# The experts' routing and weight loads move into the end of attention

## The reference, cut to what matters

```python
x = L0_attn_a_x                                    # 16 x 512 x 256
x = x + attention(layernorm(x))                    # cos/sin similarities, softmax, values
x = x + experts(layernorm(x), weights, indices)    # 2048 tokens, 2 of 8 experts each
x = x + mamba(layernorm(x))
x = x + experts(layernorm(x), weights, indices)    # the same network and the same indices

# experts: order the 4096 (token, expert) pairs by expert, then for expert e
h  = gelu(xr @ w1A[e].T @ w1B[e])                  # 256 -> 64 -> 1024
ye = h @ w2A[e].T @ w2B[e]                         # 1024 -> 64 -> 256
y[token] += expert_weight * ye
```

## Time and profile before

| | |
|---|---|
| median of three runs | 2811.41 us (2807.35 to 2814.53) |
| the profiled execution | 2807.95 us |
| its span, first to last instruction | 2805.5 us |
| PE busy | 2485.7 us (89%), x15334 |
| DVE busy | 2246.1 us (80%) |
| ACT busy | 1955.1 us (70%) |
| POOL busy | 1932.8 us (69%) |
| granted TensorE clock, mean | 0.956 |

### The profile page before, as it was taken

One profiled execution on the slowest core, in us unless ns is written; L12 is line 12 of the kernel. 1 busy time (PEld: TensorE's weight loads), 2 busy tenths in 40 slices (PEclk: granted clock), 3 DMA queues, 4 the chain that ended last, 5 costly groups with the idle time before them and its releaser, 6 DMA issues. The chain is left out here.

```text
span 2805.5 us, 42277 instructions
## 1 busy us (share of the span) xinstructions
PE 2485.7 (89%) x15334; PEld 1932.2 (69%) x15334; DVE 2246.1 (80%) x2324; ACT 1955.1 (70%) x2809; POOL 1932.8 (69%) x1245
## 2 busy tenths in 40 slices
PE   5999998399688999999999998999999999987894
PEld 4888887366266777677677776777777767767562
DVE  6788875465179898898898988999999999998554
ACT  3656564166478787787877878878889788783562
POOL 1212121142289999899999998988889889897562
PEclk9999999699799999999999999999999999999897
DMA  1212111522223042230422303303123033061234
GB/s 52 68 45 67 45 60 30 118 83 69 73 101 121 9 136 70 68 129 9 135 76 62 129 15 119 96 27 121 49 74 121 10 113 114 2 181 38 65 105 126
DMA packets 143378, 219.70 MB, mean 78 GB/s; under 512 B 27092, under 2 KB 110036, under 8 KB 143188
## 3 DMA queue, kind: packets, MB, share of 16 engines
q1 hardware_dynamic: 135028, 194.91, 22.5%
q0 software_dynamic: 8160, 22.29, 2.9%
HBM read 174.63 MB, written 42.53 MB: 77 GB/s over the span
## 5 line engine op out<-in xcount | busy, mean ns | idle before, releaser
L1508 POOL TENSOR_TENSOR m_state<-m_state,m_c_all 128x1024 f32<-128x1024 f32 x512 | 1199.3, 2365 | 139.1 <-DVE m_state L1615 138.8
L1615 DVE TENSOR_TENSOR_SCAN m_state<-m_decay,m_ps_d 128x1024 f32<-128x1024 f32 x512 | 1152.3, 2274 | 130.6 <-PE m_ps_d L1941 79.0
L1674 ACT ACTIVATE m_decay<-m_dt,m_aneg 128x511 f32<-128x511 f32 x1024 | 663.4, 710 | 20.2 <-DVE m_state L1615 19.4
L1941 PEld LDWEIGHTS m_ps_d<-m_bdiag,m_duT 128*128 128x128 f32 x4096 | 507.1, 197 | 95.6 <-issue 76.3
L1954 PE MATMUL m_ps_y<-k_ident,m_state 128*128 128x128 f32 x4096 | 526.5, 275 | 26.3 <-POOL m_state L1508 26.0
L1941 PE MATMUL m_ps_d<-m_bdiag,m_duT 128*128 128x128 f32 x4096 | 518.1, 281 | 17.6 <-DVE m_state L1615 17.3
L1954 PEld LDWEIGHTS m_ps_y<-k_ident,m_state 128*128 128x128 f32 x4096 | 469.5, 142 | 91.1 <-issue 53.0
L1603 DVE TENSOR_TENSOR m_ps_d<-m_ps_u,m_b_all 128x1024 f32<-128x1024 f32 x256 | 315.6, 1233 | 35.3 <-DMA m_b_all<-m_bc_rows 14.5
L1848 PE MATMUL m_ps_f<-k_w_2a,k_w_1b 128*128 128x512 f32 x512 | 262.6, 639 | 44.5 <-ACT m_up L1762 32.4
L1873 PE MATMUL m_ps_f<-m_up,k_w_1b 128*128 128x512 f32 x512 | 232.0, 596 | 0.7 <-ACT m_up L1762 0.7
L194 POOL TENSOR_TENSOR a_trig_lo<-a_trig,a_trig_hi 128x2048 fp32r<-128x2048 f32 x16 | 75.3, 4708 | 160.4 <-ACT a_trig_hi L356 160.4
(11 more groups left out here) (228 smaller groups left out, 4377.4 us busy)
## 6 DMA issues: line engine op xcount, KB each, us to landing
m_c_all<-m_bc_rows SPq DMA_DIRECT2D x128, 512.0 KB, 5.2
m_b_all<-m_bc_rows SPq DMA_DIRECT2D x64, 512.0 KB, 6.9
out<-m_xw SPq DMA_DIRECT2D x32, 512.0 KB, 3.3
a_xin<-x SPq DMA_DIRECT2D x16, 512.0 KB, 4.6
a_xres<-x SPq DMA_DIRECT2D x16, 512.0 KB, 5.4
x<-a_xout SPq DMA_DIRECT2D x16, 512.0 KB, 3.4
k_w_2a<-x SPq DMA_DIRECT2D x16, 512.0 KB, 8.9
m_xw<-out SPq DMA_DIRECT2D x16, 512.0 KB, 8.8
```

Source lines behind the costliest of these rows:

```text
L1508: nc.gpsimd.tensor_tensor(s, s, c_all[:, n, :, :], ALU.mult).then_inc(weighed, 1)
L1615: nc.vector.tensor_tensor_scan(state[:, r, :, :].rearrange("p n t -> p (n t)"), decay[:, r, :, :].rearrange("p n t -> p (n t)"), ps_d[i % ...
L1674: ins = nc.scalar.activation(decay[:, r, j, 1:S], dt_sb[:, c % DR, 1:S], ACT.Exp, scale=aneg[:, c, n:n + 1])
L1941: ins = nc.tensor.matmul(ps_d[1][:, j, t * P:(t + 1) * P], duT[:, c % DR, t, :], bdiag[:, n // 2, TT * j + t, :], start=True, stop=True)
```

## The change

`attention` only notes its arguments; the first `expert_ffn` calls it as `attention_stage` with the indices and sizes. The routing block and `load_weights` are gone. In their place, inside attention:
- SP loads the indices and expert numbers at the very start, ahead of the first `xin`.
- Step 14 (`NB - 2`): DVE runs `count_pairs` between the angle reduction and `xout`, PE runs the three counting products after the outputs, DVE runs `place_pairs` after `xout`.
- Step 15 (`NB - 1`): DVE runs `mark_slots` after L219, PE runs the 32 list products after the last outputs, DVE runs `list_slots` after the last `xout`. SP issues the loads of `w_2a`, `w_1a` and `w_1b` (nine DMAs) after the load of `xres`, each behind the semaphore that says that attention has no more use for the buffer; after the last store is done it stores the four lists, and waits for the nine loads.
- The instructions of the routing are the same in number, shape and order, and so are their waits on each other, but one: the count waits for all three products, not two. Small tiles of the routing lie in attention's `theta` and `turns`, the large ones in `trig_hi[0]` and `trig_lo[0]`, the products in `ps_t`.
- `w_1a`, `w_1b`, `w_2a` are buffers that outlive attention (`kept1`); `xin`, `xn`, `rest`, `sin_in` and `cos_in` of attention are views of them. The identity is loaded once.
- `w_2b` is loaded at the start of the tiles' block, by SP; PE waits for it before its first use.

```diff
+            sp.dma_start(g_i[:, :, :], indices.rearrange("(t p) k -> p t k", p=P)).then_inc(r_loaded, 16)
+            sp.dma_start(ex_sb[:, :], experts).then_inc(r_loaded, 16)
 
             def emit(st):            # SP
...
                     sp.dma_start(xres[h][:, :, :], rows(x, st.item(0))).then_inc(xres_loaded[h], 16)
+                    if isinstance(st.base, int) and st.item(0) == NB - 1:
+                        sp.wait_ge(xT_full, KT * NB)
+                        sp.dma_start(kept["w_2a"][:, :].rearrange("p (q e) -> p q e", e=ER),
+                                     ROUTE["w2aT"].rearrange("(q p) e -> p q e", p=P)).then_inc(kept_loaded, 16)
+                        sp.wait_ge(reduced, 5 * NB)
...
+                        sp.wait_ge(trig_in_used, 3 * NB)
...
             for h in range(2):
                 sp.wait_ge(stored[h], 16 * (NB // 2))
+            sp.wait_ge(r_list, 4)
+            sp.dma_start(ROUTE["slots"], slots[:, :]).then_inc(r_stored, 16)
+            sp.dma_start(ROUTE["places"], places[:, :]).then_inc(r_stored, 16)
+            sp.dma_start(ROUTE["rows"], pair_row[:, :]).then_inc(r_stored, 16)
+            sp.dma_start(ROUTE["owner"], owner[:, :]).then_inc(r_stored, 16)
+            sp.wait_ge(kept_loaded, 16 * (1 + 2 * KT + 4))
...
             def emit(st):            # DVE
...
+                if isinstance(st.base, int) and st.item(0) == NB - 2:
+                    count_pairs()
+                if isinstance(st.base, int) and st.item(0) == NB - 1:
+                    dve.wait_ge(sim_full, TT * (NB - 1))
+                    mark_slots()
...
+                if isinstance(st.base, int) and st.item(0) == NB - 2:
+                    place_pairs()
+                if isinstance(st.base, int) and st.item(0) == NB - 1:
+                    list_slots()
...
             def emit(st):            # PE, behind the outputs of the step
...
+                if isinstance(st.base, int) and st.item(0) == NB - 2:
+                    pairs = hit.rearrange("p k t e -> p (k t e)")
+                    pe.wait_ge(xT_copied, KT * NB)
+                    pe.wait_ge(r_step, 8)
+                    nc.tensor.matmul(from_p, before_p[:, :], pairs, start=True, stop=True).then_inc(r_pairs, 1)
+                    nc.tensor.matmul(from_all, ones[:, :], pairs, start=True, stop=True).then_inc(r_pairs, 1)
+                    nc.tensor.matmul(ps_t[1][:, NC * E:NC * E + 1], before_p[:, :], ones[:, 0:1], start=True,
+                                     stop=True).then_inc(r_pairs, 1)
+                if isinstance(st.base, int) and st.item(0) == NB - 1:
+                    pe.wait_ge(r_step, 31)
+                    for c in range(NC):
+                        ins = nc.tensor.matmul(from_list, is_lo[:, c, :],
+                                               tok_hi[:, c, :, :].rearrange("p a h -> p (a h)"), start=(c == 0),
+                                               stop=(c == NC - 1))
+                    ins.then_inc(r_pairs, 1)
...
             if first:                # SP in the tiles' block
+                for half in range(2):
+                    sp.dma_start(w_2b[half * R:(half + 1) * R, :, :], w2b.rearrange("(e r) d -> r e d", r=R))\
+                        .then_inc(down_loaded, 16)
```

More of the change, by code:

```diff
@@ L66, in attention, with keep @@
     PI_IN = 3.1415925
+    hold = ROUTE["hold1"] = ExitStack()
+    def keep(name, shape, dt=F32):
+        return hold.enter_context(nc.sbuf_tensor("a_" + name, shape, dt))
+    kept = ROUTE["kept1"] = {"w_1a": keep("w_1a", [P, 2 * KT * ER]), "w_1b": keep("w_1b", [P, ER * FF // P]),
+                             "w_2a": keep("w_2a", [P, FF // P * ER]), "ident": keep("ident", [P, P]),
+                             "slots": keep("slots", [P, NH], I32), "rows": keep("rows", [P, NH], I32),
+                             "places": keep("places", [P, NC], I32), "owner": keep("owner", [1, MT], I32)}
+    r_loaded, r_step, r_pairs, r_list, r_stored, kept_loaded = ROUTE["held1"] = [
+        nc.alloc_semaphore("r_" + n) for n in ("loaded", "step", "pairs", "list", "stored", "kept_loaded")]
+    ROUTE["r_stored"] = r_stored
     with ExitStack() as ctx:
@@ L108, in attention, with room @@
         rden = sb("rden", [P, TT])
+        g_i = sb("g_i", [P, NT, TOPK], I32)
+        ex_sb = sb("experts", [P, E])
+        taken = [0, 0]
+        def room(t, *shape):
+            size = math.prod(shape)
+            flat = (theta, turns)[t][:, :, :].rearrange("p f s -> p (f s)")[:, taken[t]:taken[t] + size]
+            taken[t] += size
+            names = "abcd"[:len(shape)]
+            if len(shape) == 1:
+                return flat
+            return flat.rearrange(f"p ({' '.join(names)}) -> p {' '.join(names)}", **dict(zip(names[1:], shape[1:])))
+        g_f = room(0, NT, TOPK)
+        hit = room(0, TOPK, NT, E)
+        ones, run, before_p = room(0, P), room(0, P), room(0, P)
+        zero_first, count, upto = room(0, E, NC), room(0, E, NC), room(0, E, NC)
+        place_e = room(0, NC, E)
+        tiles, ends, base = room(0, E), room(0, E), room(0, E)
+        place, row_hi, row_lo, column = room(0, NC), room(0, NC), room(0, NC), room(0, 1)
+        list_lo, list_f, token_f, later = room(0, NH), room(0, NH), room(0, NH), room(0, NH)
+        is_hi = room(1, NC, NH)
+        passed, owner_f = room(1, MT, E), room(1, MT)
+        is_lo = trig_hi[0][:, 0:NC * P // S, :].rearrange("p a (c q) -> p (a c) q", q=P)
+        tok_hi = trig_lo[0][:, :, :].rearrange("p a s -> p (a s)")[:, 0:NC * 2 * NH]\
+            .rearrange("p (c a h) -> p c a h", a=2, h=NH)
+        slots, pair_row, places, owner = kept["slots"], kept["rows"], kept["places"], kept["owner"]
         ps_t = [ctx.enter_context(nc.psum_tensor(f"a_ps_t{r}", [P, 512], F32)) for r in range(2)]
@@ L944, in ranks_in @@
             def ranks_in(j, e):
-                if j == 0 and first:
-                    act.wait_ge(w_loaded, 16 * 2 * KT)
                 if j >= 2:
@@ L1067, in _ @@
                     down(j, 0)
-    if not first:
-        ROUTE["hold"].close()
-        held.extend(ROUTE["held"])
+    ROUTE["hold1" if first else "hold"].close()
+    held.extend(ROUTE["held1" if first else "held"])
     nc.clear_and_free_semaphores(held)
```

360 lines of the change are left out of this document (148 added, 212 removed).

## The result

| | before | changed |
|---|---|---|
| median, us | 2812.55 (2803.01 to 2819.51, 8 runs) | 2792.12 (2786.12 to 2801.11, 8 runs) |
| ratio, 95% interval | | 0.9933 (0.9912 to 0.9953), some 19 us |
| profiled execution, its span | 2807.95, 2805.5 | 2791.97, 2790.2 |
| granted clock, mean | 0.956 | 0.961 |

The changed kernel was timed twice more, each time beside the kernel before on one chip: 2785.07 against 2814.89 us (ratio 0.9902, 0.9874 to 0.9929) and 2776.39 against 2800.90 us (0.9913, 0.9897 to 0.9930). The three differences are 20.4, 29.8 and 24.5 us; 24.4 was forecast. In the changed file the lines of the rows ahead are L415 (before L219), L280 (L194), L612 (L407), L635 (L430), L649 (L723), L491 (L290), L253 (L173), L453 (L257), L851 (L830), L862 (L841).

A forecast was written before the change was run, and what follows sets the result against it. A serial 32.6 us stretch between attention and the first network's tiles, a chain beside weight loads nearly as long, was taken as the bound; 29.5 - 5.0 - 0.5 - 0 = 24.0 us off 2811.4 gives 2787.4, named 2787 (range 2779 to 2796).

The forecast's parts named there:

- the tail: From PE's last output product to the tiles' first instruction: 36.7 us shrink to 7.2, gain 29.5 us.
- `place_pairs`: Behind step 14's xout: its small DVE instructions stand still while POOL's L194 runs, so L219 ends 5.0 us later.
- the gathers: Tiles' start: the 1 MB load of w_2b beside the first gathers costs 0, with 2 us as the other bound.
- start, and all before step 14: Program's start: index and expert-number loads ahead of the first xin delay all that follows by 0.5 us (bounds 0 and 2.3).
- rival A: No exclusion for small instructions: place_pairs runs beside POOL's L194; saving 28.5 us, 2783 us; chance 0.13.
- the case that the prediction had named beside the one taken: DVE's scan gets in ahead of L194, POOL starts some 0.7 us later, DVE's next instruction waits: 4.3 to 5.1 us.
- The loads: Attention's last step: nine DMAs (5.2 MB) at 198 GB/s end near 498, before the last store; cost nothing.
- Rivals C and D: C: slow loads hold the block's end, 2800 us, chance 0.04; D: loads at 70 GB/s, slower, 2822 us, chance 0.02.
- one half alone would leave the other to hold the block: Between attention and tiles, 32.6 us: chain and weight loads are nearly equally long; if one left, the other holds the block.
- Rival B: More comes back: list products at half clock, full start cost, slower gathers; saving 16.7 us, 2795 us; chance 0.12.
- Rival E: Attention's loop steps get worse, or moved work waits for something missed; about 2811 us; chance 0.03.
- What the profile would show: Signs: first statistics at about 11 us, tiles 7.2 us after PE's last output product, L219 ending 5 us later.

The follow-up runs named there:

- before_again: The kernel before, unchanged, run for a second trace: 2811.31 us in one run, tiles take 177.71 us.
- before_third: The kernel before, unchanged, run for a third trace; its tiles start at 535.01 us.
- again: The changed kernel once more, nothing edited: 2785.07 us, ratio 0.9902 to the kernel before.
- after_third: The changed kernel, unchanged, for its third trace: 2776.39 us, ratio 0.9913 to the kernel before.
- e1_place_later: The changed kernel with place_pairs moved from step 14 to behind L415 of step 15: 2784.80 us, ratio 0.9894 to the kernel before.
- e2_w2b_early: The changed kernel with w_2b loaded in attention's last step instead of at the tiles' start: 2781.34 us, ratio 0.9886 to the kernel before.
- e5_routing_only: The changed kernel with all weights loaded at the tiles' start, routing kept in attention: 2807.40 us, ratio 0.9969 to the kernel before.
- e4_loads_only: The changed kernel with routing back in its own block, the weights' loads kept in attention: 2815.80 us, ratio 0.9994 to the kernel before.

## Why the prediction was right

It was 2787.0 us from 2811.4, a gain of 24.4; the three pairs of medians gave 20.4, 29.8 and 24.5. The mechanism was right, and so was the size of the large term, the tail. `place_pairs` was taken 0.6 us too high, the gathers were mis-sized, and one small term was missing. Means over the three traces of each kernel (before, `before_again`, `before_third`; changed, `again`, `after_third`), in us:

| step | predicted | measured |
|---|---|---|
| last output to tiles | 36.7 to 7.2, gain 29.5 | 36.9 to 7.7, gain 29.2 |
| `place_pairs` beside POOL | -5.0 | -4.4 |
| L415's end to the last output | not in the sum | +0.6 |
| start, and all before step 14 | -0.5 | -0.1 |
| tiles' start | 24.0 earlier | 25.4 earlier |
| `w_2b` beside the gathers | 0, bound -2 | -2.5 to -2.9 |

By the traces the change is worth 25.4 - 2.5 to 2.9, some 22.7 us, where the sum said 24.0. Part of that closeness is luck: the gathers cost more, `place_pairs` and the start cost less, and the clock gave something back. The medians can't tell 22.7 from 24.4, since their three differences lie 9 us apart. The start of the tiles itself lies 2.4 us apart in three traces of the changed kernel, so the smallest terms are no finer than that.

*The tail.* The list products ended 3.57 us behind the outputs, as forecast. The margin was thin: the granted clock is 1.00 up to 504.7 and 0.50 from there, and the last product ends at 504.96; in the other two traces it falls 0.25 and 0.46 us ahead of that end. The forecast rested on the clock at 499 to 500 alone. SP stored the lists at once: the last store had landed at 505.12, 1.3 us before they were ready. The tail is 0.5 us longer than forecast, and 0.4 of that lie behind the lists: SP's four issues and the block's end took 2.57 us instead of 2.19.

*`place_pairs`.* The mechanism was right, for the smallest instructions too, and rival A (no exclusion for them) is refuted by the 4.29 us of L329 and by `e1_place_later`. The size fell to the case that the prediction had named beside the one taken: the scan got in first, POOL started late (4.81 us instead of 4.50 long), and the next instruction waited. That case was given as 4.3 to 5.1 and measured 4.37. The rule of the Trainium skill ("SBUF — State Buffer", Who interferes with whom) is that whoever issues first holds the shared ports for its whole instruction and the other is blocked. The trace agrees in both orders: the scan held L280 back, then L280 held back a DVE instruction of eight elements.

*The 0.6 us.* PE's chain from L415's end to the last output shrank from 21.47 to 20.83 us (means of three). The clock returned to 1.00 sooner: the similarities ran at half clock for 5.1 us after PE's wait in the profile of before (477.58 to 482.6) and for 3.5 us in the changed kernel's (480.72 to 484.2). Stretches with the return in them, before and changed, columns as in the earlier trace rows:

```profile
480.60:483.60 3.00, 3.00 (x10) 2.35 (x10) 0.00 (x0) 0.61 (x1) 0.00 (x0) 0.66 0.00 0
```
```profile
483.80:486.80 3.00, 3.00 (x14) 2.46 (x13) 3.00 (x2) 1.39 (x2) 0.00 (x0) 0.93 1.06 223
```

This was no step of mine, and no run shows that the change earns it. In `e2_w2b_early`, where `place_pairs` stands as in the changed kernel, the half clock lasted 4.7 us and the chain took 21.43.

*The start.* First statistics at 10.04 us; the forecast was 11 or so. The two small loads took SP 1.85 us, not 2.3, and DVE was busy with the weights up to 10.12 us. In three traces each the first statistics start at 10.2 us on average before and at 10.4 in the changed kernel.

*The loads.* Over before 496 us, forecast 498; no wait. Rivals C and D had the loads holding the end of the block; here the engines moved 264 GB/s from 470 to 492. `e5_routing_only` shows the price of the loads where they are not hidden: 15 us. The claim that one half alone would leave the other to hold the block is borne out in full by `e4_loads_only` and in part by `e5_routing_only`, where the weights held the first tiles for 15 of the 26.5 us.

*The gathers, the step that was mis-sized.* I took 0 because 1 MB at 198 GB/s is over in 5.3 us, before DVE's second look at 7.5 us. But the first look comes at 5.0 us, and PE's first transposes hang on it. It came 3.3 us late, the second followed it and came 2.0 us late, PE's first transpose as well, and 2.5 to 2.9 us stayed in the tiles: more than the bound of 2. The Trainium skill ("DMA: Bandwidth & Descriptors", Queues, rings and completion order) has a DMA engine take turns between queues by packet; that the gathers finished 3.3 us late and not 5.3 fits that, and does not make it free. So does `e5_routing_only`: with all the weights on SP's queue the first statistics came 7.57 us behind the start, sooner than the 8.3 us beside 1 MB.

*Rival B* (16.7 us) came nearest in this term, with 2 us, and had the other two wrong. *Rival E*, the loop's steps: all instances of L415, columns as in the earlier trace rows,

```profile
L415 DVE TENSOR_TENSOR a_trig_lo<-a_trig,a_trig_hi x16: 2277/2279/3205, 51.0 to 478.3; 128x2048 fp32r<-128x2048 f32 x16
```

have the median of L219, and the statistics have a median of 409 ns in both kernels. *What the profile would show* came as written but for three numbers: the statistics at 10.0 us and not 11, the tail of 7.7 us and not 7.2, and L415's end 4.4 us later against POOL's L280 and not 5.

*Slips in the working.* The chances of the forecast, A, B and C add up to 0.95, not 0.94. And `mark_slots` is 8.7 us by the rows that were cited, not 9.5 (it took 9.49). Neither moves the forecast.

*A warning about the size.* One trace of each kernel would have misled: the first pair has 10.3 us more in the tiles after the change, of which 2.5 are the change's. Only the second trace of before showed that. Whether the timed runs behind the first pair of medians differed in the same way isn't known: three of the eight runs of before are older than the rest. In the other two pairs both kernels were timed together, and they gave 29.8 and 24.5 us.

## What to carry to other kernels

Where a serial stretch is held by two chains of like length (here a 32 us chain of small instructions and 26 us of loads), moving either alone gives little (2 and 10 us), moving both gives most of the stretch (some 24 us): price the halves before judging one. Small DVE instructions were not free beside a GpSimd tensor_tensor (4.4 us); put them behind the instruction that the critical path waits for. When a stage that the edit does not touch grows by several us, take the trace of the unchanged kernel again on the same chip before looking for a cause in the edit.

## What the runs showed of the hardware that I had not expected

- A DVE tensor_scalar of 8 elements took 4.29 us instead of 0.17 beside a POOL tensor_tensor of 2048 elements, and POOL's own lasted 4.81 instead of 4.50 us when a DVE scan had got in first.
- A 1 MB load on SP's queue beside POOL's first indirect gathers delayed the first gathered tile's use by 3.3 us (8.29 instead of 4.96).
- The same kernel's tiles took 169.2 us or 177.7 us, with 37 of PE's semaphores late in the longer form (most by up to 1.5 us), alike for all kernels timed together.
- The changed kernel's mamba layer, which no edit touches, took 1892.7 to 1898.0 us, with the experiments 1889.0 to 1903.9: a spread wider than either of the two small edits was worth.
